# Reordering VectorE's work in the combining stage of a two-layer attention and expert kernel

## The reference, cut to what matters

```
xn = layernorm(x);  s = attention0(xn);  g = silu(experts0(xn));  x = x + s * g
xn = layernorm(x);  s = attention1(xn);  g = silu(ffn1(xn));      x = x + s * g
```

```
experts0:    ... + silu(xn @ sw_gate) * (xn @ sw_up) @ sw_down      # shared expert, 704 wide
layer 0 end: x = x + s * silu(routed + shared);  xn = layernorm(x)
attention1:  K, V = rotary((layernorm'(xn) @ W_in + b_in)[K, V columns])
             A = sum over tokens of  (K / |K|) * (V / |V|)          # one row of 512 per batch
```

## Time and profile before

| | |
|---|---|
| median of three runs | 4155.71 us |
| the profiled execution's own time | 4156.09 us |
| span in its profile | 4154.3 us |
| TensorE busy | 3936.8 us, 95% of the span |
| VectorE busy | 2134.2 us, 51% |
| ScalarE busy | 1654.7 us, 40% |
| GpSimd busy | 1406.4 us, 34% |
| mean granted TensorE clock | 0.982 |

### The profile page before, as it was taken

How to read it: one execution, slowest core, us unless ns; L and a number is a source line. 1 busy time by engine, 2 the same in 40 slices (tenths; PEclk the granted TensorE clock), 3 DMA queues, 4 the chain that set the end, 5 groups by cost and what they waited for, 6 DMA issues and landing times. The chain is left out here.

```text
span 4154.3 us, 67670 instructions
## 1 busy us (share of the span) xinstructions
PE 3936.8 (95%) x22285; PEld 3413.7 (82%) x22286; DVE 2134.2 (51%) x4225; ACT 1654.7 (40%) x3268; POOL 1406.4 (34%) x2073
## 2 busy tenths in 40 slices
PE   8969998899999999999997999998999999999998
PEld 6757777899899999989885888876788888788887
DVE  7778887444444444444436566564333334233333
ACT  3357776344334444434333434333322222222222
POOL 0045555555555555555550343443000000000000
PEclk9979999999999999999998999999999999999999
DMA  9989874565556565556645545443333133132221
GB/s 340 355 197 205 181 152 104 134 131 126 117 117 132 126 132 127 119 123 132 141 72 193 172 165 174 147 155 109 98 105 104 59 106 110 54 102 82 81 86 43
DMA packets 352043, 561.45 MB, mean 135 GB/s; under 512 B 33217, under 2 KB 198753, under 8 KB 347618
## 3 DMA queue, kind: packets, MB, share of 16 engines
q1 hardware_dynamic: 282898, 394.19, 32.0%
q0 software_dynamic: 68944, 164.62, 18.6%
HBM read 384.36 MB, written 174.34 MB: 134 GB/s over the span
## 5 line engine op out<-in xcount | busy, mean ns | idle before, releaser
L2486 POOL DMA_DIRECT2D out<-d_res x32 | 17.4, 543 | 1253.9 <-DVE d_res L2722 1253.9
L1321 POOL DMA_INDIRECT acc_d<-e_yw,e_to x208 | 336.1, 1616 | 286.6 <-ACT e_yw L1478 270.1
L2668 DVE TENSOR_TENSOR d_h<-d_sg,d_psU 128x512 f32<-128x512 f32 x136 | 93.5, 688 | 508.7 <-PE d_psU L108 450.0
L1540 DVE TENSOR_TENSOR e_h<-e_sg,e_psU 128x352 f32<-128x352 f32 x208 | 108.3, 521 | 397.5 <-ACT e_sg L1491 393.8
L106 PE MATMUL e_psG<-e_gu,e_xT 128*128 128x352 f32 x832 | 290.0, 349 | 11.9 <-DVE e_xT L1532 11.8
L107 PE MATMUL e_psG<-e_gu,e_xT 128*128 128x352 f32 x832 | 272.7, 328 | 0.0
L108 PE MATMUL e_psG<-e_gu,e_xT 128*128 128x352 f32 x832 | 271.4, 326 | 0.0
L106 PE MATMUL e_psU<-e_gu,e_xT 128*128 128x352 f32 x832 | 270.1, 325 | 0.0
L107 PE MATMUL e_psU<-e_gu,e_xT 128*128 128x352 f32 x832 | 269.4, 324 | 0.0
L1291 POOL DMA_INDIRECT e_xs<-xn_d,e_idx x209 | 210.4, 1007 | 170.8 <-POOL e_idx L1288 165.7
L108 PE MATMUL e_psU<-e_gu,e_xT 128*128 128x352 f32 x832 | 266.1, 320 | 0.0
(11 more groups left out here) (462 smaller groups left out, 11782.3 us busy)
## 6 DMA issues: line engine op xcount, KB each, us to landing
b_gu_raw<-in_wgu SPq DMA_DIRECT2D x116, 512.0 KB, 3.7
d_gu_raw<-in_wgu SPq DMA_DIRECT2D x68, 512.0 KB, 3.2
a_q<-qk_d SPq DMA_DIRECT2D x96, 256.0 KB
a_k<-qk_d SPq DMA_DIRECT2D x96, 256.0 KB, 4.7
e_rawgu<-in_w_gate SPq DMA_DIRECT2D x32, 704.0 KB, 6.1
e_rawgu<-in_w_up SPq DMA_DIRECT2D x32, 704.0 KB, 6.0
xT_d<-f_xT SPq DMA_DIRECT2D x16, 1024.0 KB, 9.0
qk_d<-f_q SPq DMA_DIRECT2D x16, 1024.0 KB, 6.5
```

What stands on the lines that cost most here:

```text
L1321: pool.indirect_dma_start(env.acc_d, bass.IndirectOffsetOnAxis(ap=to[:, :].bitcast(U32), axis=0), yw[:, :], None, compute_op=ALU.add).then ...
L1540: dve.tensor_tensor(hv[:, :], sg[:, :], psU[:, 0:M], ALU.mult).then_inc(h_ready, 1)
L2668: ins = dve.tensor_tensor(hv[q % 2][:, :], sg[q % 2][:, :], psU[:, :], ALU.mult)
```

## The change

VectorE's loop in `phase_mix` is the only code that changes. No instruction is added or dropped; two places get another order.

At `k` = 4 the groups in `after` are taken in falling order of `rel`. The elder group's `last_keys` and `keys(t, 0)` stand ahead of the younger's two `residual` calls. It applies in passes 2 to 8, seven times.

For the last group all four `add` calls are made at `rel` 27, ahead of `product(QS + 7)`. Before, the product came first, then one `add` at each of `rel` 27 to 30.

`fold(k)` is called a few lines earlier. It is called in pass 0 alone, where none of the calls that it passes is made.

```
                 s = tail_at(g, after)
+                if g == 0:
+                    fold(k)
+                if g is None and s == ADD_AT:
+                    for j in range(GT):
+                        add(TILES - GT + j)
                 if s in UP:
                     product(QS + UP[s])
                 if s in LOWER:
                     gu_lower(QS + LOWER[s])
-                if g == 0:
-                    fold(k)
-                for n, rel in after:
+                for n, rel in sorted(after, key=lambda a: -a[1]) if k == 4 else after:
                     if rel == SUM_AT:
                         sums(n)
...
-                    if ADD_AT <= rel < ADD_AT + GT:
+                    if ADD_AT <= rel < ADD_AT + GT and n < GROUPS - 1:
                         add(GT * n + rel - ADD_AT)
```

## The result

The kernel after takes 4127.04 us (median of 6 runs, 4124.42 to 4132.68), the kernel before 4156.53 us (6 runs). The medians lie 29.5 us apart. The ratio that the runs give is 0.9934, with a 95% interval from 0.9925 to 0.9944: 27.4 us less, and 23 to 31 by the interval. I go by the ratio, which the traces bear out. The forecast was 4130 us, 26 us less.

The account below looks back on a forecast made before the run. TensorE was taken to bound the combining stage. The terms 13.2 + 6.3 + 2.1 + 4.3 = 25.9 us, off the profiled 4156.09, gave 4130.2, forecast as 4130 us, own range 4126 to 4135.

Parts of the forecast that it names:

- The wait in passes 2 to 7: TensorE's six waits for VectorE to take the keys out vanish whole: 6 x 2.2 = 13.2 us, bounds 11.4 and 13.8.
- The margin of VectorE at the keys: In step 5 TensorE completes the keys 0.06 us before VectorE's third key instruction starts, so VectorE isn't held up.
- the slack at step 11: Tightest meeting point, TensorE's next `last_keys` needing `x_lower`: slack 2.33 us before the change, 0.13 after.
- The clock: The 1.2 GHz stretches behind four of TensorE's six waits go with them: 4 x 1.57 = 6.3 us, bounds 0 and 9.4.
- Rival A: The clock loss stays in passes 2 to 7 however TensorE is fed: gain 19.6, 4136.5 us; chance 0.11.
- Pass 8: TensorE's keys start 3.17 us earlier, 1.1 lost to VectorE instructions held by GpSimd: 2.1 us, bounds 1.0 and 3.2.
- The last sums: At the phase's end, sums ahead of the last product let `similar` start 4.3 us earlier; bounds 3.4 and 6.
- B: Part given back at step 11: `x_lower` chain 1 us later, TensorE stands still 0.9 us a pass, 4139 us; chance 0.11.
- C: `kv_ready` was not what held TensorE, so only the change to the last sums gains: 4152 us; chance 0.03.
- D: Slower: VectorE reaches step 5 early and waits for TensorE's keys, residuals up to 3.8 us late: 4164 us; chance 0.03.
- The stage's clock: Sign that the forecast is right: the granted clock of the combining stage is 0.99 and not 0.97.

Follow-up runs that it names:

- the run with the keys alone: Kernel before with only the elder group's keys put ahead of the residuals in passes 2 to 8, last sums unmoved: 4128.73 us, ratio 0.9944 to before.
- the delay of `x_lower`: Kernel after with one more 0.73 us VectorE instruction, result unused, just ahead of `x_lower` in passes 2 to 7: 4128.69 us, ratio 0.9941 to before.
- sums only: Kernel before with only the four last sums put ahead of the last product, keys still behind the residuals: 4149.75 us, ratio 0.9992 to before.
- x_lower late by three: Kernel after with three more VectorE instructions, 2.19 us, just ahead of `x_lower` in passes 2 to 7: 4144.85 us, ratio 0.9977 to before.

## Why the prediction was right

**The wait in passes 2 to 7.** Forecast 13.2 us. The period fell from 73.77 to 71.53, 6 x 2.24 = 13.4 us. The margin of VectorE at the keys was forecast at 0.06 and is 0.07 us, the slack at step 11 at 0.13 and is 0.21 by the same rows, 0.14 by the delay of `x_lower`. Shown by the run with the keys alone and by the delay of `x_lower`.

**The clock.** Forecast 6.3 us. From the second gate product of pass 2 (at 2335.74 and 2335.95) to the last down product of pass 7 (2768.50 and 2748.89) the traces have 432.76 and 412.94 us, 19.8 us apart; less the 13.4 it is 6.4. The cause was argued then and is shown now. Stops of 1.90 to 2.06 us brought a slow stretch in 14 passes of 18 (before, sums only, x_lower late by three), stops of 3.15 and 4.22 us in 11 of 12, stops of under 0.5 us in none of 12, and without a stop there was none in 30. Rival A has fallen. That four of the six passes of before would be slow was read from its trace; the execution with the sums only had five, so that this term came within 0.1 us is in part luck. The Trainium skill ("TensorE: Matmul & The Clock Gate", "Why this matters for your kernels") warns of long gaps only; here stops of 1.90 to 2.06 us, which it does not warn of, cost about 1.5 us more in most cases. In one point its account fits: by the section "What's actually happening" the gate's check runs free of the kernel, and equal stops do differ in whether a slow stretch follows.

**Pass 8.** Forecast 2.1 us, measured 2.6 (78.62 and 76.06 us from the last down product of pass 7 to a gate product of pass 9, at 2847.12 and 2824.95). The keys came the full 3.17 us earlier. About 1 us was given back, as forecast: the chain of small instructions from L2139 to L2159 took 4.73 us and not 3.70. The one that forms the factor took 1.11 us, the next but one 0.58, and each ends within 0.03 us of the end of a GpSimd instruction. That GpSimd holds them is argued from this; no run took its work away. But the loss did not reach the transposes, which came 3.1 us earlier; it went into a new wait of 0.54 us for `gu_lower`, and the gate product behind them came 2.2 us earlier:

```profile
2785.16 1.11 PE L1866 MATMUL c_psX<-ident,c_xn 128*128 128x128 f32 x4 [4.95 <-ACT c_xn L1991]
2786.81 0.80 PE L106 MATMUL b_psG<-b_x,b_gu 128*128 128x512 f32 x1 [0.54 <-DVE b_gu L2084]
```

Some tenths came back from a slow stretch that was two matmuls shorter.

**The last sums.** Forecast 4.3 us; 4.3 measured up to the reduction (27.49 and 23.19 us from the mark in pass 9), and 0.4 more since the reduction's small matmuls run faster right behind others (0.95 us, not 1.33).

**Sum.** 25.9 forecast, 27.2 in the traces, 27.4 in the runs. The forecast's terms are each within 0.5 us. Rivals B, C and D did not come; the runs show that B and D name real mechanisms, with 0.14 us and one step of distance to them. One sign was missed. The stage's clock was to be 0.99 and is 0.98: it is 1.00 from 2286 to 2750 us, but 0.89 in the 106 us ahead of that and 0.97 in the 102 behind, where the change leaves the slow stretches.

## What to carry to other kernels

Where one engine's stream sets the time, look for its waits and then at what the engine waited for was doing while the data lay ready. Moving short instructions ahead of long ones in an in-order engine is worth the wait and, for TensorE, the slow clock behind it where the wait is long enough to bring it (here 1.90 us was, 0.45 us was not). Count two margins before moving: whether the data are there when the moved instruction comes (one step too early made this kernel 0.15% slower than before), and which meeting point has the least slack once the bounding engine runs ahead.

## What the runs showed of the hardware that I had not expected

A stop of TensorE of 2.04 us costs 2.24 us for itself and, in most cases, 1.5 to 1.6 us of slow clock; with 4.22 us the slow clock alone cost 2.5 us in most passes, with 0.44 us nothing. A stop's price is not linear in its length.

Where TensorE starts again after even a short wait, it loses about 0.26 us more than the idle time that the profile shows (0.70 for 0.44). Of this 0.16 us is only in the way the profile draws a matmul's end, and 0.10 us is the first matmul's.
